# Context and key/value weights as pairs of f16 instead of pairs of float32r in the cross attention's projection

## What is computed

```
x = x + _L0_xattn_ref(_layernorm(x, axis=-1), ctx_2048, L0_xattn_Wq, L0_xattn_Wk, L0_xattn_Wv)

q = x @ Wq.T
k_raw = context @ Wk.T          # 2048 x 256 keys per batch, values alike with Wv
# q and k_raw: 32 heads of 8, each head divided by its root mean square (EPS = 1e-06)
# softmax over the 2048 keys, scaled by 8 ** -0.5, then the weighted sum of the values
```

## Time and profile before

| what | value |
|---|---|
| time of 3 runs | 412.41 us median (410.93 to 414.05) |
| profiled execution | 411.95 us, its span 410.4 us |
| granted TensorE clock, mean | 0.996 of full |
| TensorE busy | 382.4 us (93% of the span) |
| VectorE busy | 325.6 us (79%) |
| ScalarE busy | 267.1 us (65%) |
| GpSimd busy | 224.4 us (55%) |

### The profile page before, as it was taken

How to read it: one execution, slowest core, us unless ns; L and a number is a source line. 1 busy time by engine, 2 the same in 40 slices (tenths; PEclk the granted TensorE clock), 3 DMA queues, 4 the chain that set the end, 5 groups by cost and what they waited for, 6 DMA issues and landing times.

```text
span 410.4 us, 14567 instructions
## 1 busy us (share of the span) xinstructions
PE 382.4 (93%) x6055; PEld 303.8 (74%) x6055; DVE 325.6 (79%) x736; ACT 267.1 (65%) x554; POOL 224.4 (55%) x286
## 2 busy tenths in 40 slices
PE   7889989999999999889999999999889988799996
PEld 5557767777677777669999998777778865567775
DVE  7777989998688788766999996786997757866763
ACT  3578888898888888985554543640999445444542
POOL 3466687666566676104755440441199753999800
PEclk9999999999999999999999999999999999999999
DMA  5637741542221110271000008030000193000000
GB/s 163 232 117 236 237 131 48 183 143 72 85 87 37 31 30 4 105 279 57 2 2 1 2 1 347 7 141 2 2 2 2 30 384 159 1 2 2 0 2 26
DMA packets 10832, 34.78 MB, mean 85 GB/s; under 512 B 2192, under 2 KB 7312, under 8 KB 8976
## 3 DMA queue, kind: packets, MB, share of 16 engines
q1 hardware_dynamic: 10624, 33.86, 24.0%
q10 hardware_dynamic: 144, 0.00, 0.0%
HBM read 33.60 MB, written 0.26 MB: 83 GB/s over the span
## 4 chain that ended last, share of the span: by engine, by line
PE 52%; DVE 21%; POOL 10%; issue 9%; ACT 5%; DMA 1%; SPq 0%; DVEq 0%; POOLq 0%; ACTq 0%
PE ps L1895 10%; PE ps L1852 7%; PE ps L1263 6%; PE ps L1245 5%; PE ps L1882 3%; PE ps L974 3%; PE ps L956 3%; PE ps L1865 2%; PE ps L472 2%; POOL sb_halves L1694 2%; PE ps L915 2%; ACT sb_arena L1803 2%; PE ps L922 2%; DVE sb_big L653 2%; POOL sb_uacc L1707 1%
## 5 line engine op out<-in xcount | busy, mean ns | idle before, releaser
L1803 ACT ACTIVATE sb_arena<-ps 128x1024 f32<-128x1024 f32 x128 | 123.8, 1020 | 20.2 <-PE ps L1882 19.3
L1895 PE MATMUL ps<-sb_arena 128*25 128x128 f32 (+1 forms) x2048 | 70.5, 275 | 1.9 <-issue 1.5
L1895 PEld LDWEIGHTS ps<-sb_arena 128*25 128x25 f32 (+1 forms) x2048 | 50.8, 97 | 10.6 <-issue 2.7
L1852 PE MATMUL ps<-sb_halves 128*128 128x512 f32 x192 | 54.0, 417 | 2.3 <-POOL sb_halves L1694 1.4
L562 POOL TENSOR_TENSOR sb_halves<-sb_big,sb_halves 128x256 fp32r<-128x256 f32 x28 | 21.6, 791 | 44.4 <-ACT sb_halves L546 44.4
L1685 POOL TENSOR_TENSOR sb_big<-sb_arena 128x256 f32<-128x256 f32 x30 | 18.7, 624 | 49.0 <-DVE sb_arena L1562 49.0
L1852 PEld LDWEIGHTS ps<-sb_halves 128*128 128x128 f32 x192 | 34.1, 191 | 15.1 <-issue 6.0
L1174 POOL TENSOR_TENSOR sb_mid<-sb_mid 128x512 f32<-128x512 f32 x16 | 21.9, 1378 | 20.3 <-DVE sb_mid L1074 20.2
L1337 ACT ACTIVATE sb_arena<-ps 128x176 f32<-128x176 f32 x40 | 12.5, 318 | 28.5 <-PE ps L1263 28.5
L1882 PE MATMUL ps<-sb_w_ri,sb_arena 32*128 32x128 f16 x1024 | 26.3, 218 | 3.3 <-ACT sb_arena L1803 1.3
L1442 DVE SCALAR_TENSOR_TENSOR sb_arena<-ps,sb_w_q,sb_arena 128x176 f32<-128x176 f32 x40 | 15.4, 395 | 17.5 <-ACT sb_arena L1337 17.3
(11 more groups left out here) (269 smaller groups left out, 930.2 us busy)
## 6 DMA issues: line engine op xcount, KB each, us to landing
sb_arena<-in_ctx SPq DMA_DIRECT2D x32, 128.0 KB, 2.8
sb_mid<-in_w_down SPq DMA_DIRECT2D x1, 3584.0 KB, 12.6
sb_big<-in_w_gu SPq DMA_DIRECT2D x1, 3520.0 KB, 11.8
sb_mid<-in_w_ffn SPq DMA_DIRECT2D x3, 768.0 KB, 4.4
sb_big<-in_w_gu SPq DMA_DIRECT2D x1, 2112.0 KB, 7.5
sb_big<-in_w_q SPq DMA_DIRECT2D x2, 1024.0 KB, 5.1
sb_big<-in_w_k SPq DMA_DIRECT2D x2, 1024.0 KB, 6.6
sb_big<-in_w_v SPq DMA_DIRECT2D x2, 1024.0 KB, 5.5
```

Source lines behind the costliest of these rows:

```text
L1803: nc.scalar.activation(probs[:, n % P_SLOTS].rearrange("p a g n -> p a (g n)"), ps[:, bank:bank + 2], ACT.Exp, scale=XD ** -0.5).then_inc( ...
L1852: i = T.matmul(ps[:, 7], ctx_half[:, t % 2, c, kt], wkv_half[:, d, kt], start=(n + kt == 0), stop=(n == 2 and kt == KT - 1))
L1895: i = T.matmul(ps[32 * gg:32 * gg + m, 6, j * P:(j + 1) * P], v_sb[:, t % V_SLOTS, 4 * gg + j, head], probs[:, n % P_SLOTS, a, gg], start= ...
```

## The change

The split parts become f16 numbers. `wkv_half` and `ctx_half` move from the tile `halves` (float32r) into the part of `w_ri` that is free during the cross attention (its first part holds `qT_x` already; the weights that belong into `w_ri` are loaded when the last scores are done, before and after). The key/value weights are multiplied by W_SCALE = 256 before they are split. So keys and values come out 256 times larger: the keys' division by their root mean square takes that out, with its small constant multiplied by 256 squared, and the column of ones beside the values becomes a column of 256, so the softmax's division takes it out of the values. The six matmuls, and every engine's list of instructions with its waits, stay the same in number and order; line numbers grow by one or two. ScalarE's first split of the weights is an activation with a scale instead of a cast, and VectorE's is a scalar_tensor_tensor instead of a tensor_tensor.

```diff
--- before.py
+++ after.py
@@ -132,8 +132,9 @@
 
 
         halves = sb("halves", [P, 4096], F32R)
-        wkv_half = halves[:, 0:2048].rearrange("p (c k n) -> p c k n", c=2, k=KT)
-        ctx_half = halves[:, 2048:3072].rearrange("p (s c k m) -> p s c k m", s=2, c=2, k=KT)
+        x_pairs = w_ri[:].rearrange("p c t n -> p (c t n)")
+        wkv_half = x_pairs[:, 1024:2048].bitcast(F16).rearrange("p (c k n) -> p c k n", c=2, k=KT)
+        ctx_half = x_pairs[:, 2048:2560].bitcast(F16).rearrange("p (s c k m) -> p s c k m", s=2, c=2, k=KT)
         HALF_PRODUCTS = ((0, 0), (1, 0), (0, 1))
 
 
@@ -1512,8 +1513,8 @@
             V.memset(xnT[:, :, :, 0:3], 0.0)
             V.memset(v_sb, 0.0).then_inc(sem("v_cleared"), 1)
             dve.wait_ge(sem("v_cleared"), 1)
-            V.memset(v_sb[:, :, :, 8:9], 1.0)
-            V.memset(v_sb[:, :, :, 33:34], 1.0)
+            V.memset(v_sb[:, :, :, 8:9], W_SCALE)
+            V.memset(v_sb[:, :, :, 33:34], W_SCALE)
             dve.wait_ge(sem("x_loaded"), 16)
             layer_norm(dve, LN_OF["xattn"])
 
@@ -1611,7 +1612,8 @@
             decay_rate()
             ln_copy(dve, 0, 0)
             dve.wait_ge(sem("wkv_high"), 1)
-            V.tensor_tensor(wkv_half[:, 1], w_xkv, wkv_half[:, 0].bitcast(F32), ALU.subtract).then_inc(sem("wkv_split"), 1)
+            V.scalar_tensor_tensor(wkv_half[:, 1], w_xkv, W_SCALE, wkv_half[:, 0], ALU.mult, ALU.subtract
+                                   ).then_inc(sem("wkv_split"), 1)
             decay_weights(0)
             decay_weights(1)
             mean_squares_q(0)
@@ -1691,7 +1693,7 @@
                     pool.wait_ge(sem("kv_projected"), t - 1)
                 G.tensor_copy(ctx_half[:, t % 2, 0], ctxT[:, t % CTX_SLOTS]).then_inc(sem("ctx_high"), 1)
                 pool.wait_ge(sem("ctx_high"), t + 1)
-                G.tensor_tensor(ctx_half[:, t % 2, 1], ctxT[:, t % CTX_SLOTS], ctx_half[:, t % 2, 0].bitcast(F32),
+                G.tensor_tensor(ctx_half[:, t % 2, 1], ctxT[:, t % CTX_SLOTS], ctx_half[:, t % 2, 0],
                                 ALU.subtract).then_inc(sem("ctx_split"), 1)
 
             def weigh_context(t):
@@ -1753,7 +1755,7 @@
             nc.scalar.activation(dec[:, 0:1], decay[:], ACT.Exp, scale=-1.0).then_inc(sem("decay_exp"), 1)
 
             act.wait_ge(sem("wkv_loaded"), 16)
-            nc.scalar.copy(wkv_half[:, 0], w_xkv).then_inc(sem("wkv_high"), 1)
+            nc.scalar.activation(wkv_half[:, 0], w_xkv, ACT.Copy, scale=W_SCALE).then_inc(sem("wkv_high"), 1)
 
             def take_queries(b):
                 act.wait_ge(sem("q_projected"), b + 1)
@@ -1790,7 +1792,7 @@
 
             def key_rstd(t):
                 act.wait_ge(sem("k_meansq"), t + 1)
-                nc.scalar.activation(kln, kms[:, t % 2], ACT.Ln, bias=1e-6, scale=1.0 / XD).then_inc(sem("k_log"), 1)
+                nc.scalar.activation(kln, kms[:, t % 2], ACT.Ln, bias=1e-6 * W_SCALE ** 2, scale=1.0 / XD).then_inc(sem("k_log"), 1)
                 act.wait_ge(sem("k_log"), t + 1)
                 nc.scalar.activation(krs[:, t % 2], kln, ACT.Exp, scale=-0.5).then_inc(sem("k_rstd"), 1)
```

## The result

The changed kernel took **408.44 us** (median of 4 runs, 407.55 to 409.00), the kernel before 412.89 (4 runs, 410.93 to 414.05): a ratio of **0.9887, 95% interval 0.9843 to 0.9931**, 1.1% faster. All 16 runs together have a mean of 410.0, the 84 runs of the kernel before that were made beside the experiments 412.7: 2.7 us, where 2.75 were forecast. Whether the change itself makes the lower clock more frequent, these runs do not decide. The profiled execution took 408.89 us, its span 407.3, at a granted clock of 1.00.

What follows compares the result with a forecast made beforehand. Two loops, TensorE's (4.71 us) and GpSimd's with VectorE's cast (4.70), bound the context projection; first stretch 0.65, second 0.9, last cycle 0.2, start 0.6 and halts 0.4 make 2.75, so 411.95 becomes 409.2 us, range 406.0 to 412.8.

Steps and rivals of the forecast that it cites:

- two loops: Projection cycles late in the context loop: TensorE's own 4.71 us and GpSimd's with VectorE's cast, 4.70, bound them together.
- Six matmuls in f16: TensorE's projection of each of 32 context tiles: 0.2 us shorter, between bounds of 0.1 and 0.29.
- GpSimd's cast unchanged, the subtraction 0.06 shorter: GpSimd's split of the next context tile: cast stays at 397 ns, subtraction falls from 728 to 660.
- The second rival: GpSimd's time goes by the element, so neither split instruction gets cheaper: 1.3 us gained, 410.6 us; chance 17%.
- First stretch 0.65: Projection cycles from 36.14 to 91.74 us, where GpSimd's loop is longer: 11 cycles by 0.06 us.
- Second stretch, typical cycles: Projection cycles from 91.74 to 165.32 us: 0.07 us off the 4.71 in 13 cycles, 0.9 us together.
- Halts made good, 0.4 us for two, and 0.2 in the last cycle: TensorE's 0.3 us lead recovers part of two mid-group halts; the last cycle, without GpSimd's split, gains the projection's 0.2.
- The start, 0.6: Three projections before 36.14 us, where VectorE waits for the projection: 0.6 us gained.
- Weights, once, covered: ScalarE's and VectorE's new weight-split forms at the start keep their length and end before GpSimd's first subtraction: no cost.
- The first rival: TensorE's gain comes through, as VectorE's key scaling issues ahead of GpSimd and its cast ends earlier: 406.2 us; chance 25%.
- the third rival: GpSimd's split gets dearer, cast up 0.196 us, lengthening 24 cycles by 0.136 each: 414.3 us, slower; chance 9%.
- One sign that was named: Profile after, 110 to 160 us: TensorE waits ahead of the key transposes, as it does before 90 us.

Runs made afterwards that it cites:

- the four matmuls: Changed kernel with four instead of six projection matmuls per context tile from the third on (product with the weights' low half left out): 406.27 us, 0.9855 of the kernel before.
- the split alone: Kernel before with GpSimd's context split in f16 from the third tile on, written to a place the float32r matmuls don't read: 412.83 us, 1.0005.
- the split ahead: Changed kernel with a third place for the context pairs and GpSimd's whole split moved behind the weighing, a tile earlier: 416.49 us, 1.0078.
- the longer subtraction: Changed kernel with GpSimd's subtraction cut into two instructions of 128 elements: 410.51 us, 0.9945 of the kernel before.
- the moved cast: Changed kernel with GpSimd's cast of the next context tile moved ahead of the square of the keys: 414.17 us, 1.0036 of the kernel before.

## Why the prediction was right, and what in it was not

The forecast of 409.2 us lies between the two medians measured, 408.44 and 411.14, and its mechanism held: two loops, of which TensorE's gets 0.2 shorter and the other, GpSimd's, 0.06. Point by point:

- *Six matmuls in f16, 0.2 us each*: 0.19 measured (1.59 to 1.40).
- *GpSimd's cast unchanged, the subtraction 0.06 shorter*: 400 and 674 ns, 0.054 shorter. The second rival (time by the element) fell with that. "GPSIMD Engine Reference", section "Elementwise — side-by-side cycle accounting", of the Trainium skill counts some 2.6 cycles per element for two inputs and names no width. That doesn't hold for this pair of forms: 728 ns became 674 with an f16 operand and result.
- *First stretch 0.65*: 0.70. *Second stretch, typical cycles*: 0.07 said, 0.09 measured (4.71 to 4.62). Both are near the forecast, and the four matmuls show that more speed on TensorE is worth nothing there.
- *Halts made good, 0.4 us for two, and 0.2 in the last cycle* is the mis-sized term. The last cycle gave 0.38 (4.70 to 4.32), since TensorE brought its whole lead of 0.33 into it. The five cycles with halts took 25.05 us before and 23.97 after (109.55 to 133.52), 1.08 less, of which 0.45 are five times the typical 0.09 and 0.6 are halts. The cycle in which GpSimd adds nothing up (from 89.67) gave another 0.15, TensorE's gain, which the sum did not have. So the second stretch gave 2.32 where 1.5 were said.
- *The start, 0.6*: 0.70 where it was meant. The three cycles from the first copy of the keys to the stretch took 14.46 us (20.31 to 34.77), 15.16 before (20.98 to 36.14), and the third of them, which ends with VectorE waiting for the projection, 5.02 in place of 5.41. That repeats: it takes 5.41 and 5.42 in the two other profiles with float32r matmuls, and 4.96 to 5.23 in all with six in f16. Another 0.67 came before the first copy and is the luck of two executions. Before, the third projection ran at a granted clock of 0.57 and took 2.67 us (from 18.27), after, 1.47 at full clock; against that the first one started 0.75 later (9.72 us, 8.97 before), waiting for GpSimd's first split, which waited for the tile's load and began at 7.7 (6.9 before). Such a slow early projection is in profiles of either format (2.58 with the split alone, 2.27 with the split ahead).
- *Weights, once, covered*: VectorE's new form took 1.45 us (1.32 before) and ended at 9.14, GpSimd's first subtraction at 9.67.
- Of the 4.39 us that this profile had gained by the end of the loop, 1.3 were lost in the stage of the last weights, by the order of GpSimd and VectorE, which the prediction didn't have and the change doesn't cause.
- The first rival, that TensorE's gain comes through, is nearer than its 25% said: not in the typical cycles of the changed kernel, but by way of the halts, and by the flip of order that it named, which the longer subtraction and the moved cast both showed. Against the third rival, a dearer split, stands the cast of 400 ns; and its rule that a longer split lengthens every cycle held, with the longer subtraction, in the second stretch alone.
- One sign that was named didn't come: TensorE does not wait ahead of the key transposes between 110 and 160 us (its only waits there are two halts of 0.3), and it is busy for 98% of the second stretch as before. That it is ahead shows only in the projection, which is done 0.32 us before it is taken; the wait itself shows with four matmuls.

What I missed is a third limit beside the two loops, as I infer TensorE's supply of instructions. It doesn't show in the changed kernel, where GpSimd's loop sets the pace, and it took the gain of each kernel that moved GpSimd's work forward.

## What to carry to other kernels

Where two loops of nearly equal length bound a stage, shortening one gains what the other leaves in a typical cycle, and a lead out of which that engine pays its own halts; both are to be counted, and halts are found as cycles that are longer than their neighbours. Where VectorE and GpSimd hold each other up, ask who is issued first at each meeting, since a shift of 0.02 to 0.06 us moves half a microsecond from one to the other. Work that ends earlier also starts its transfers earlier: look at what the loads that it releases then stand in front of, instruction blocks included.

## What the runs showed of the hardware

- TensorE halts for 1.5 to 2.1 us in the middle of a group when a 16 KB block of instructions is late beside a weight load of a megabyte (that the block is TensorE's is inferred); without the loads the long halts before 60 us are gone, with half the size one of 1.5 us is left. The granted clock was 0.83 from 40 to 50 us, behind the first halt with the cast first, and 1.00 from 50 to 70 us, behind the other two.
- VectorE's cast of 128x256 takes 0.29 us alone and 0.63 when it meets GpSimd's addition; a VectorE tensor_tensor of the same size 0.42 and 0.95. GpSimd's multiplication is held up in turn, 0.98 in place of 0.73 us. This agrees with the Trainium skill, "SBUF — State Buffer", section "Who interferes with whom": VectorE in a two-port mode, or with both inputs in SBUF, contends with GpSimd for a shared pair of ports, and the order of issue decides who waits.
- What f16 saves in a group of six matmuls with 512 columns: they follow one another at 0.216 us (0.232 in float32r), and the second follows the first after 0.227 in place of 0.338; the weight loads take 98 ns in place of 188. 0.11 and five times 0.016 make the 0.19.
